# A graph layer's edge stage: edges in stored order and added to DRAM tables, in place of a sort by destination and an SBUF accumulator

## The reference, cut to what matters

```python
def _L0_gnn_ref(node_feat, edge_feat, src, dst, We1, be1, We2, be2, Wn1, bn1, Wn2, bn2, eps):
    e = _mlp2(edge_feat, We1, be1, We2, be2)              # 40000 x 256 -> 512 -> 256
    msg = relu(node_feat[src] + e)
    out_h = segment_sum(msg, dst, num_segments=2500)
    return _mlp2((1.0 + eps[0]) * node_feat + out_h, Wn1, bn1, Wn2, bn2)

x = x + _L0_gnn_ref(_layernorm(x), edge_attr_256, src, dst, ...)
```

## Time and profile before

| | us |
|---|---|
| median of 3 runs without the profiler (3002.5 to 3002.54) | 3002.51 |
| span of the profiled execution, first to last instruction | 3198.3 |
| of it: until the first hidden product of the edge stage | 319.5 |
| of it: from there to the end of the edge stage | 1243.8 |
| of it: from the node MLP to the end | 1635.0 |

### The profile page before, as it was taken

How to read it: one execution, slowest core, us unless ns; L and a number is a source line. 1 busy time by engine, 2 the same in 40 slices (tenths; PEclk the granted TensorE clock), 3 DMA queues, 4 the chain that set the end, 5 groups by cost and what they waited for, 6 DMA issues and landing times. The chain is left out here.

```text
span 3198.3 us, 54121 instructions
## 1 busy us (share of the span) xinstructions
PE 2348.5 (73%) x14408; PEld 1941.4 (61%) x14409; DVE 1951.0 (61%) x5493; ACT 1141.6 (36%) x2522; POOL 1194.9 (37%) x1158
## 2 busy tenths in 40 slices
PE   0994899999999999999743499997125556554676
PEld 0331788888888888888743388886124434443565
DVE  7997566666566666666683644444445555556773
ACT  0994334343343343434320155554011222212221
POOL 0001555555555555655000011111536676663000
PEclk9997899999999999999875699999567676766787
DMA  0001222222222222223100367675222233225000
GB/s 39 0 0 56 75 72 68 70 74 71 72 69 69 72 71 67 76 69 73 26 0 32 114 235 248 237 246 173 61 72 81 78 88 85 79 83 48 19 8 32
DMA packets 129241, 256.68 MB, mean 80 GB/s; under 512 B 26393, under 2 KB 64326, under 8 KB 128563
## 3 DMA queue, kind: packets, MB, share of 16 engines
q0 software_dynamic: 56480, 145.84, 17.1%
q1 hardware_dynamic: 72708, 110.19, 10.1%
HBM read 238.57 MB, written 17.34 MB: 80 GB/s over the span
## 5 line engine op out<-in xcount | busy, mean ns | idle before, releaser
L455 POOL DMA_INDIRECT edge_ea<-in_edge_attr_dram,edge_edge_idx x332 | 339.8, 1023 | 611.7 <-DVE edge_edge_idx L615 520.8
L578 ACT ACTIVATE edge_whole<-edge_h_ps,edge_b 128x512 f32<-128x512 f32 x332 | 227.3, 685 | 655.5 <-PE edge_h_ps L374 385.1
L1594 POOL DMA_INDIRECT att_got<-head_table,att_idx x352 | 372.0, 1057 | 225.3 <-issue 115.4
L461 POOL DMA_INDIRECT edge_nf<-node_table,edge_node_idx x332 | 359.4, 1082 | 221.0 <-DVE edge_node_idx L618 111.8
L373 PE MATMUL edge_e_ps<-edge_w_low,edge_hid_high 128*128 128x256 f32 x1328 | 375.0, 282 | 7.4 <-issue 7.3
L374 PE MATMUL edge_e_ps<-edge_w_high,edge_hid_high 128*128 128x256 f32 x1328 | 374.1, 282 | 8.3 <-issue 7.9
L372 PE MATMUL edge_e_ps<-edge_w_high,edge_hid_low 128*128 128x256 f32 x1328 | 375.3, 283 | 5.5 <-issue 5.1
L372 PE MATMUL edge_h_ps<-edge_eat_high,edge_w_low 128*128 128x512 f32 x664 | 280.1, 422 | 53.2 <-ACT edge_whole L578 45.6
L631 DVE TENSOR_TENSOR edge_hid_low<-edge_whole,edge_hid_high 128x512 fp32r<-128x512 f32 x332 | 231.8, 698 | 83.0 <-ACT edge_hid_high L583 42.6
L373 PE MATMUL edge_h_ps<-edge_eat_low,edge_w_high 128*128 128x512 f32 x664 | 276.5, 416 | 6.0 <-issue 6.0
L374 PE MATMUL edge_h_ps<-edge_eat_high,edge_w_high 128*128 128x512 f32 x664 | 275.7, 415 | 2.7 <-issue 2.5
(11 more groups left out here) (380 smaller groups left out, 5231.5 us busy)
## 6 DMA issues: line engine op xcount, KB each, us to landing
moe_w<-in_L_ffn_w_dram SPq DMA_DIRECT2D x162, 512.0 KB, 4.8
routed<-moe_out SPq DMA_DIRECT2D x54, 128.0 KB, 6.2
att_got<-head_table,att_idx POOLq DMA_INDIRECT x352
edge_ea<-in_edge_attr_dram,edge_edge_idx POOLq DMA_INDIRECT x332
edge_nf<-node_table,edge_node_idx POOLq DMA_INDIRECT x332
head_table<-hrow_rows SPq DMA_DIRECT2D x1, 2519.5 KB
x<-in_x_dram SPq DMA_DIRECT2D x1, 2500.0 KB
node_table<-edge_table_rows SPq DMA_DIRECT2D x1, 2500.0 KB
```

What stands on the lines that cost most here:

```text
L455: nc.gpsimd.indirect_dma_start(ea[u][:, j, :], None, io["edge_attr_256"][:, :], bass.IndirectOffsetOnAxis(ap=edge_idx[u][:, j:j + 1], axis ...
L461: nc.gpsimd.indirect_dma_start(nf[u][:, j, :], None, m.node_table[:, :], bass.IndirectOffsetOnAxis(ap=node_idx[u][:, j:j + 1], axis=0)).th ...
L578: act.activation(whole[c][:], h_ps[:, c % 2, :], ACT.Relu, bias=b1[:, c:c + 1]).then_inc(hid_whole, 1)
L1594: pool.indirect_dma_start(got[v][:, j, :], None, m.head_table[:, :], bass.IndirectOffsetOnAxis(ap=idx[v][:, j:j + 1], axis=0)).then_inc(la ...
```

## The change

The sort by destination goes, with its tables. Edges are taken in their own order: lane p holds edges 320p to 320p+319, and a group is four columns of 125 edges, 80 groups in all.

- Edge rows are plain loads on SyncE's queue: per group 4 KB of each lane, in two DMAs (lanes 0 to 111 and 112 to 124, `SPLIT`). The same queue brings the destinations of the group's 500 edges to all partitions (`dst_row`), from a DRAM copy `dst_rows` that is written in the stage's beginning.
- GpSimd still gathers the node rows, now 125 at a time.
- `find_same` on VectorE compares the 125 destinations of a column with each other: `same[e, f]` is 1 where edges e and f have one destination. TensorE multiplies it with the messages (`gather_same`), so each edge's row holds the sum over all edges of the column with its destination. ScalarE copies these sums to `agg` (`take_sums`).
- `find_same` also counts, for each edge, the earlier ones of the column with the same destination, and `find_slots` makes an index: the destination for the first of them, a row past the table's 2500 for the others.
- GpSimd adds the 125 rows of `agg` to a DRAM table by an indirect DMA with add. Columns 0 and 2 of a group go to table 0, columns 1 and 3 to table 1. Before an add GpSimd waits until the last add to the same table has landed.
- Table 0 is first written with `(1+eps)*y`, table 1 with zeros. At the end `node_mlp` loads both tables and adds them, in place of `combine`'s multiply-add of `y` and `acc`.
- The layer norm, the input loads and the weights' splitting move into the edge stage's block, and a few of them from VectorE to ScalarE (high parts of the weights). Large loads and stores of 125 lanes are cut by `SPLIT`, except the zeros of table 1. Semaphores of the stage are cleared and freed after it.

```diff
+SUMS = 2
+EVEN = 112
+SPLIT = (slice(0, EVEN), slice(EVEN, LANES))
...
-    groups = EDGE_BLOCKS // G
+    groups = EDGE_COLS // G
...
+                def load_edges(u, g):
+                    for lanes in SPLIT:
+                        sp.dma_start(ea[u][lanes], edges[lanes, bass.DynSlice(g * G, G), :]).then_inc(ea_landed[u], 16)
+
+                def load_dst(u, g):
+                    sp.dma_start(dst_row[u][:], m.dst_rows[bass.DynSlice(g * N, N)].partition_broadcast(P)).then_inc(dst_landed[u], 16)
+
+                def refill(u, g):
+                    sp.wait_ge(turned, g - 1)
+                    load_edges(u, g)
+                    sp.wait_ge(repeats_found, g - 1)
+                    load_dst(u, g)
...
+                sp.wait_ge(table_ready, 1)
+                for lanes in SPLIT:
+                    sp.dma_start(m.node_table.rearrange("(p t) d -> p t d", t=TILES)[lanes], table_rows[lanes]).then_inc(table_stored, 16)
+                sp.wait_ge(rows_stored, 48)
+                for u in range(2):
+                    load_dst(u, u)
+                sp.wait_ge(own_ready, 1)
+                for lanes in SPLIT:
+                    sp.dma_start(m.sums[0][0:N_NODES, :].rearrange("(p t) d -> p t d", t=TILES)[lanes], own_rows[lanes]).then_inc(sums_begun, 16)
+                sp.wait_ge(zeros_ready, 1)
+                for k in range(SUMS):
+                    sp.dma_start(m.sums[k][N_NODES:N_NODES + LANES, :], zeros[:]).then_inc(sums_begun, 16)
+                for k in range(1, SUMS):
+                    sp.dma_start(m.sums[k][0:N_NODES, :].rearrange("(p t) d -> p t d", t=TILES),
+                                 zeros[:].unsqueeze(1).to_broadcast([LANES, TILES, DIM])).then_inc(sums_begun, 16)
+                with sp.Fori(1, groups // 2) as turn:
+                    for u in range(2):
+                        refill(u, turn * 2 + u)
+                for k in range(SUMS):
+                    sp.wait_ge(sum_landed[k], groups * (G // SUMS) * 16)
...
-                def edges_then_nodes(g, u, wait_summed):
-                    pool.wait_ge(edge_idx_ready, g + (u + 1))
-                    pool.wait_ge(turned, g + (u - 1))
-                    gather_edges(u)
-                    pool.wait_ge(node_idx_ready, g + u)
-                    if wait_summed:
-                        pool.wait_ge(summed, g + (u - 2))
-                    gather_nodes(1 - u)
+                def add_sums(g, u, n, first=False):
+                    for k in range(SUMS):
+                        j = n * SUMS + k
+                        if not (first and n == 0):
+                            pool.wait_ge(sum_landed[k], g * (16 * G // SUMS) + 16 * n)
+                        own_waits(pool, m)
+                        pool.indirect_dma_start(m.sums[k][:, :], bass.IndirectOffsetOnAxis(ap=slot[u][:, j:j + 1], axis=0),
+                                                agg[u][:, j, :], None, compute_op=ALU.add).then_inc(sum_landed[k], 16)
+
+                def one_group(g, u, first=False, ahead=True):
+                    pool.wait_ge(slot_ready, g + 1)
+                    pool.wait_ge(agg_ready, g + 1)
+                    for n in range(G // SUMS):
+                        add_sums(g, u, n, first)
+                        if ahead:
+                            if n == 0:
+                                pool.wait_ge(node_idx_ready, g + 3)
+                                pool.wait_ge(summed, g + 1)
+                            gather_nodes(u, range(n * SUMS, (n + 1) * SUMS))
...
+            def take_sums(g, u, first=False):
+                act = nc.scalar
+                act.wait_ge(gathered, g + 2)
+                if not first:
+                    for k in range(SUMS):
+                        act.wait_ge(sum_landed[k], g * (16 * G // SUMS) - (16 * G // SUMS))
+                act.activation(agg[u][:], s_ps[0:LANES, :, :], ACT.Copy).then_inc(agg_ready, 1)
...
-            def accumulate(g, j, tile, first=False):
-                if not first or j > 0:
-                    nc.vector.wait_ge(added, g * G + j)
-                nc.vector.tensor_tensor(m.acc[:, tile, :], s_ps[0:LANES, j, :], m.acc[:, tile, :], ALU.add).then_inc(added, 1)
+            def find_same(u, g, first=False):
+                nc.vector.wait_ge(dst_landed[u], (g - u) * 8 + 16)
+                if not first:
+                    nc.vector.wait_ge(gathered, g)
+                for j in range(G):
+                    last = nc.vector.tensor_scalar(same[u][:, j, 0:LANES], dst_row[u][0:LANES, j * LANES:(j + 1) * LANES],
+                                                   dst[:, bass.DynSlice(g * G + j, 1)], None, ALU.is_equal)
+                last.then_inc(same_ready, 1)
+                for j in range(G):
+                    last = nc.vector.scalar_tensor_tensor(before[:, j, :], dst_row[u][0:LANES, j * LANES:(j + 1) * LANES],
+                                                          dst[:, bass.DynSlice(g * G + j, 1)], m.earlier[:], ALU.is_equal, ALU.mult,
+                                                          accum_out=repeats[:, j:j + 1])
+                last.then_inc(repeats_found, 1)
+
+            def find_slots(u, g, first=False):
+                nc.vector.wait_ge(repeats_found, g + 1)
+                nc.vector.scalar_tensor_tensor(moves[:], repeats[:], 0.0, move[:, cols], ALU.is_gt, ALU.mult).then_inc(moves_found, 1)
+                nc.vector.wait_ge(moves_found, g + 2)
+                if not first:
+                    for k in range(SUMS):
+                        nc.vector.wait_ge(sum_landed[k], g * (16 * G // SUMS) - (16 * G // SUMS))
+                nc.vector.tensor_tensor(slot[u][:], moves[:], dst[:, cols], ALU.add).then_inc(slot_ready, 1)
...
                     hidden_low(g, 3)
-                    dve.wait_ge(scattered, g)
-                    accumulate(g - 1, 0, tiles[0], first)
...
                     if ahead > 0:
                         eat_low(g + 1)
+                    find_same(u, g, first)
+                    find_slots(u, g, first)
...
 def node_mlp(nc, sem, m, io):
+                for part, tiles in enumerate((slice(0, 2 * ST), slice(2 * ST, TILES))):
+                    for k in range(SUMS):
+                        for lanes in SPLIT:
+                            sp.dma_start(sums[k][lanes, tiles, :], m.sums[k][0:N_NODES, :].rearrange("(p t) d -> p t d", t=TILES)[lanes, tiles, :]
+                                         ).then_inc(sums_in[part], 16)
                 sp.dma_start(w1[:], io["Wn1"].rearrange("(k p) h -> p k h", p=P)).then_inc(w_in, 16)
...
-                    nc.vector.scalar_tensor_tensor(z[u][:], m.y[:, tiles, :], eps1[:, 0:1], m.acc[:, tiles, :],
-                                                   ALU.mult, ALU.add).then_inc(z_ready, 1)
+                    if isinstance(n, int) and n in (0, 2):
+                        dve.wait_ge(sums_in[n // 2], SUMS * 32)
+                    nc.vector.tensor_tensor(z[u][:], sums[0][:, tiles, :], sums[1][:, tiles, :], ALU.add).then_inc(z_ready, 1)
```

More of the change, by code:

```diff
@@ L1 @@
-from contextlib import ExitStack
+from contextlib import ExitStack, contextmanager
 import concourse.bass as bass
@@ L411, in sb, with two @@
             return ctx.enter_context(nc.sbuf_tensor(f"edge_{n}", shape, dt))
+        def two(n, shape, dt=F32):
+            return [sb(f"{n}{u}", shape, dt) for u in range(2)]
         def parts(n, shape):
@@ new lines, in _ @@
+                pool.memset(zeros[:], 0.0).then_inc(zeros_ready, 1)
+                pool.wait_ge(table_stored, 32)
+                for u in range(2):
+                    pool.wait_ge(node_idx_ready, u + 1)
+                    gather_nodes(u, range(G))
+                pool.wait_ge(sums_begun, 32 + 16 * (2 * SUMS - 1))
+                one_group(0, 0, first=True)
+                one_group(1, 1)
+                with pool.Fori(1, groups // 2 - 1) as turn:
+                    for u in range(2):
+                        one_group(turn * 2 + u, u)
@@ L495, in transposes @@
+                for u in range(2):
+                    one_group(groups - 2 + u, u, ahead=False)
             def transposes(u, landed):
@@ new lines, in _ @@
+                dve.wait_ge(high_split, 1)
+                nc.vector.tensor_tensor(w1l[:], w1[:], w1h[:].bitcast(F32), ALU.subtract).then_inc(weights_split, 1)
+                dve.wait_ge(gathered, 1)
+                for n, cut in enumerate(cuts):
+                    last = nc.vector.tensor_copy(dst_t[0:cut.stop - cut.start, n, :], s_ps[0:cut.stop - cut.start, n, 0:LANES])
+                last.then_inc(rows_made, 1)
+                dve.wait_ge(m.x_landed, 32)
+                for t in range(TILES):
+                    last = nc.vector.bn_stats(m.stats[:, t, :], m.x[:, t, :])
@@ new lines, in _ @@
+                chain.link(last)
+                for t in range(TILES):
+                    last = nc.vector.bn_aggr(mv[:, t, :], m.stats[:, t, :])
+                chain.link(last)
```

(16 more changed lines are left out.)

340 lines of the change are left out of this document (159 added, 181 removed).

## The result

The changed kernel takes 3045.1 us (median of 4 runs, 3041.9 to 3051.0) against 3002.5 before: a ratio of 1.0143 (95% interval 1.0129 to 1.0158), slower by 42.6 us. The forecast was 2792, the range 2685 to 3010. The profiled execution took 3051.0 us at a span of 3049.2, so this profile isn't stretched as the one of before was.

What follows compares the result with a forecast made beforehand. GpSimd was to bound the edge loop at 14.2 us a group, over TensorE's 13.1. Stage end 1444.8 - 1219.3 = 225.5 us saved, less 15.2 in the node MLP: 3002.5 - 210.3 = 2792 us, range 2685 to 3010.

Steps and rivals of the forecast that it cites:

- stage end of 1219.3: Edge stage's end in the changed kernel: 82 + 79 x 14.2 + 14.9 + 0.6 = 1219.3 us.
- The start: Before the edge loop: first hidden product at 44 us, both tables written and GpSimd's loop starting at 82.
- The period: Edge loop: 14.2 us per group, two waves of 7.1 on GpSimd, over TensorE's 13.1.
- rival 3: Edge loop: add instruction dearer on GpSimd; 2840 us at 1.8 us, near 3095 at twice a gather's; 0.19 shared with rival 2.
- The last adds: Edge stage's end: a wave of 7.1 us, 1.6 for the second table, 6.2 to land, 0.6 for the barrier.
- The landing: Edge loop: an add, counted from its issue's start, lands after 6.2 us, taken from a plain store's landing.
- TensorE's own pace: Edge loop: 80 groups of 500 columns at 13.1 us each on TensorE.
- Rival 2: Edge loop: adds land late, no gain from period 16.8 us on, 3448 us at landing 10.3; 0.19 shared with rival 3.
- The base: Kernel before without the profiler: 13.3 us a group, 118.5 us of stalls taken off, edge stage ending at 1444.8.
- The node MLP: Node MLP's start: loads of two tables stand ahead of the weights on SyncE's queue, 15.2 us lost.
- The attention layer: After the edge stage: counted in the 1635.0 us not touched but for the node MLP's start.

Runs made afterwards that it cites:

- before with 43 groups: The kernel before with 43 of its 83 edge groups, the other 40 groups' edges left out: 2474.7 us.
- both padded: The changed kernel with gathers and adds made on 128 rows instead of 125: 2840.8 us.

## Why the prediction was wrong

The forecast's stage end of 1219.3 against the measured 1425.4 makes 206.1 us; by its own terms:

- **The start, +30.5.** The first add was forecast at 82 and came at 112.5. Three sizes and one queue were off. The first hidden product came at 55.6 for 44: the weights' high parts were estimated within 27 us at the latest and began at 29.4. The node table was stored in 14.5 us (53.2 to 67.7) where the cut was to bring 24.0 down to 7.6. And the zeros, uncut, took from 68.9 to about 100 (the DMA share is 0.34 until then), 31 us for 24. What I had missed is who waits for them. I charged them to GpSimd's first add, and to TensorE 11 us at most. But the edge load of group 2 stands behind them on SyncE's queue, and TensorE idled for 31.5 us. The kernels with early zeros, cut by lanes, have their first add at 89.0 and 82.4. The cut itself works: the share is 0.34 of 16 engines, 5.4, with 125 lanes, and 0.96 at 102 us. The Trainium skill ("DMA: Bandwidth & Descriptors", "Why a DMA increments its semaphore by 16 and not by 1") has a rule that fits: a DMA uses the largest number of engines up to 16 that divides its slowest dimension on both sides, so 5 for 125 lanes and 16 for 112.
- **The period, +173.3.** From the first add to the first add of the last group (1407.56) it is 1295.1 us, 79 x 16.4 where 79 x 14.2 were forecast. The step that failed is the one sentence "That an add takes GpSimd the time of a gather is an assumption": 2.14 us where 1.3 was counted (1.60 with the gap). A wave is then 2 x 2.44 + 2 x 1.57 = 8.0 and the period 16.0; the landings add 0.4. The term was named as an assumption and then given no bounds of its own in the sum; only rival 3 priced it, at 1.8 and at twice the gather's 1.3, and the measured value lies between. With the period alone put right the same sum gives 2792 + 173 = 2965 us, still a gain; the other terms here and below turn it into a loss.
- **The last adds, +2.3**: 17.8 us from there to the node MLP's first load, for 15.5.

The landing came out right, 6.4 us at the median for 6.2, but by luck: the 6.2 was that of a plain store, and here a plain write landed in 4.5 and an add of 128 rows in 4.7. What the forecast made of it was wrong: a wave was to last for the landing and its lag, 6.4 + 0.9 = 7.3 by the measured landing, and GpSimd's own instructions take 8.0. Had the add been as cheap as a gather, the landing would have decided, as the kernel with plain writes shows. GpSimd as the bound was right, and so was TensorE's own pace at 13 (12.9 without adds). Rival 2, a late landing, fell. Rival 3, the dearer instruction, is what happened; it shared 0.19 with rival 2, because nothing in the trace of before was near an indirect add. The rows held a warning, though no bound: a 125-row gather took 0.25 us more than one of 128 rows, at equal bytes per row. So the instruction's time follows something other than bytes, and nothing said that an add would stay at a gather's price.

The Trainium skill ("DMA: Bandwidth & Descriptors", "Anatomy of one DMA — SWDGE (gpsimd) path") fits a DMA issued by GpSimd as 2.0 us plus bytes/436e3, 2.3 us here. As an estimate, behind the measured instruction that gives 2.14 + 2.3 = 4.4 us for an add of 125 rows and 1.72 + 2.3 = 4.0 for one of 128. They landed in 6.4 and 4.7, so both are later than the rule, the first by 2.0 us.

Outside the changed stage's end:

- **The base, +23.0.** 13.3 us a group was right (13.25 from two medians), and so was the reading of the stalls. But I took them from the stage's intervals only. The profiled execution was slow in its start too (first add of node rows at 345.1 for 334.1 with 43 groups), and the rest is the period, 13.15 in that profile for 13.3. The stage before ended at 1421.8, not at 1444.8. Against it the changed stage ends 3.6 us later. Its first add of node rows comes 250.9 us earlier (83.2 for 334.1), but the groups give back 221 (80 x 16.4 for 83 x 13.15), and most of the rest is TensorE's idle of 31.5 us in the start.
- **The node MLP, +9.4.** From its first load to its last product it takes 98.5 us for 73.9 before, 24.6 lost where 15.2 were taken. The weights stand behind eight loads of tables and are split 28.2 us after the first load for 5.3; and the first product, which once needed only SBUF, now waits for a table.
- **The attention layer, +17.9**, forecast as untouched. Its code is the same, but from its first product to its last it takes 526.5 us where before with 43 groups takes 508.6. The pages' rows of its gathers, of before with 43 groups

```profile
L1594 POOL DMA_INDIRECT att_got<-head_table,att_idx x352 | 391.2, 1111 | 143.6 <-issue 107.0
```

and of the changed kernel

```profile
L1678 POOL DMA_INDIRECT att_got<-head_table,att_idx x352 | 408.4, 1160 | 143.7 <-issue 107.0
```

  differ by 17.2 us, and in the other kernels the stage follows the same row (1116 ns and 510.6 us with four tables and gathers of 128 rows; 1152 ns and 522.6 us with both padded). So the time is in GpSimd's instructions. Most of these gathers take 0.95 to 1.0 us and some about 2.05; of the 352, 45 are such long ones in before with 43 groups and 57 in the changed kernel, and that makes most of the difference. What makes a gather a long one, and why one program has more of them, stays open.

206.1 + 23.0 + 9.4 + 17.9 = 256.4, of 258.8 between the forecast and the profiled execution. So the sort went, and the new edge stage with its start takes as long as the sort and the old stage together; the loss of 42.6 us comes from the node MLP's start and the attention layer.

## What to carry to other kernels

A DMA has three prices, and each set a pace somewhere in this case: the instruction on the engine that issues it, the landing, and what stands behind it on the queue. Where no row shows the instruction, its price needs bounds of its own and a measurement before anything is built on it. Try indirect transfers at 128 rows where a kernel has 125, with spare rows gathered or zeros added past the table's end: here that was worth 204 us. When one cause is taken away, look for the next just below it: the landing ate most of what cheaper gathers promised, and 1.6 us a group of what plain writes did.

## What the runs showed of the hardware

- An indirect add to DRAM of 125 rows of 1 KB holds GpSimd for 2.14 us and lands after 6.4; a plain indirect write 1.37 and 4.5; a gather 1.27 and 4.4. With 128 rows the add takes 1.72 and 4.7, the gather 1.03.
- The add of 125 rows makes 416 packets, the one of 128 rows 144, the write of 125 rows 128, and a gather of 128 rows 80 fewer than one of 125.
- The same gather took 1.11 to 1.17 us on average in programs that differ only elsewhere (1.06 in the stretched execution of before), by more or fewer single ones of about 2.05 us.
- One profiled execution (that of before) was 195.8 us longer than the median, by stalls on all engines. Against a profile of before with 43 groups it lost 11 us up to the first add of node rows, 131 us in the 82 intervals of the groups (14.7 us for 13.15) and 52 us from the node MLP on; that second profile showed no such stalls.
